# A two-layer relational graph network on one core: edge rows issued by ScalarE, a third stream written as plain blocks, and x halves ahead of the blocks

## The chip, the core and the metric

The kernel runs on one core of one Trainium2 chip. Five engines of the core matter here: TensorE (PE; its weight loads are PEld), VectorE (DVE), ScalarE (ACT), GpSimd (POOL) and SyncE (SP). Sixteen DMA engines move data between HBM and the on-chip memories for all of them. The metric is the device time of one execution in microseconds, and lower is better.

## The reference

Inputs: `x` (50000 x 128), 50000 edges with source `src`, destination `dst` (sorted), a type out of 8 and a row of attributes, and per layer eight weight matrices, a root matrix, a bias and batch-norm parameters.

```python
def _rgcn_edge_conv(h, xe, src, dst, etype, w, rt, b):
    m = jax.nn.relu(h[src] + xe)
    seg = etype * n + dst
    sums = segment_sum(m, seg, R * n)
    cnt = segment_sum(ones, seg, R * n)
    mean = sums / maximum(cnt, 1.0)[:, None]
    out = einsum('rnd,rdo->no', mean.reshape(R, n, -1), w)
    return out + h @ rt + b

h = maximum(_layernorm(x), 0.0)
for l in range(2):
    h = _rgcn_edge_conv(h, xe, src, dst, edge_type, weight[l], root[l], bias[l])
    h = _batch_norm(h, gamma[l], beta[l])
    if l == 0: h = relu(h)
return x + h
```

## The kernel before

**Tiles, groups, streams.** The edges are cut into 394 tiles of 127 edges. Group g (99 of them) takes one tile of each of four streams: tiles g, 99+g, 198+g and 297+g. For each group and layer: POOL gathers the source rows of each tile with an indirect DMA (L864, into one of 20 slots `hb` in layer 0, of 9 in layer 1); the group's edge rows are loaded into one of `XB` = 4 slots `xb` (`edge_rows`, L716, 256 KB); ScalarE normalises the rows (L1499, layer 0 only); VectorE adds both (L1211 in layer 0; L1214, L1215, L1217 in layer 1) and builds two selection matrices (`columns` L1228, `same_node` L1263); TensorE transposes and sorts by type (`turn`, L1749), multiplies by the weights (`products`, L1783) and sums by node (`node_sums`, L1819 and, for tiles of over 127 destination rows, L1824); ScalarE copies between (L1519, L1528, L1537), carries a node that goes on into the next tile (L1550), and copies the sums to one of `OB` = 3 slots `ob` (`sums_out`, L1562 and L1563).

**How the sums leave.** A tile's sums go to the accumulator `acc` in HBM in one of two ways. In general POOL writes 128 rows with an indirect DMA (`scatter`, L879). Where destinations are dense, a tile t covers at most `WROWS[t]` = 27/32 t + 16 rows in a row, and SP writes them as plain blocks (`window_rows`): up to 127 rows at L746, and what is beyond 127 at L749. `SPANS` lists the tiles for which that holds: 1 to 95 and 100 to 194, in the first two streams. A later block overwrites the rows that an earlier one of its stream wrote too far, so each block waits for its stream's block before to have landed (`wide_out`). `further(g)` lists the streams of a group whose tile has over 127 rows; for each, PE makes one more product (L1824), DVE one more 128 columns in L1263, and ScalarE copies 128 more columns (L1562). From group 33 on, the second stream's first block has 127 rows.

**The order of SP's queue.** In step n of a layer SP loads the first rows of group n-7's blocks into registers (`window_firsts`), issues the edge rows of group n, waits for `ob_ready` of group n-7 and issues its blocks, and then (layer 0) issues the load of half a chunk of `x` (`eh`, L766, 256 KB) that VectorE takes in the same group (L1185), and the store of the normalised half of five groups before (L730). The halves are spare work of layer 0: nearly every group from 21 on has one, before that every second. In layer 1 SP also loads chunks of 512 KB every fourth group. `sums_out` of group g waits until the blocks and scatters of group g-3 have landed.

**The loop of layer 0.** `columns` of group i+3 waits for TensorE's small products `place_column` of group i+1 (L1769), which follow `products` and, before it, `node_sums`; that waits for `same_node`, which VectorE makes after `columns`.

Of the kernel before, what the change touches and what calls it, by code (L numbers as in the profile page):

```python
# [6 lines left out]
P = 128  # L7
# [10 lines left out]
def wait(eng, sem, value):  # L18

    if value > 0:  # L20
        eng.wait_ge(sem, value)
# [20 lines left out]
def gnn_kernel(nc, x, src, dst, edge_attr, edge_type, weight, root, bias, gamma, beta, out):  # L42
    N, D = x.shape
# [6 lines left out]
    F = -(-N // (P * CW)) * CW  # L50
# [14 lines left out]
    T = P - 1  # L65
# [6 lines left out]
    NG = -(-NT // H)  # L72
# [4 lines left out]
    HB, XB, SM, OB = 20, 4, 2, 3  # L77
# [8 lines left out]
    MT, LAG = 3, 7  # L86
# [33 lines left out]
    def tiles(g):  # L120
        return [s * NG + g for s in range(H) if s * NG + g < NT]

    SPANS = ((1, NG - 4), (NG + 1, 2 * NG - 4))
    GROW, LEAST = 27.0 / 32.0, 15
    WIDE = [t for a, b in SPANS for t in range(a, b + 1)]
    WROWS = {t: int(GROW * t) + LEAST + 1 for t in WIDE}
    WB = WIDE[-1] // P + 1
# [11 lines left out]
    def in_window(g):  # L139

        return [t for t in tiles(g) if t in WIDE]
# [17 lines left out]
    with ctx:  # L159
# [509 lines left out]
        def xb_parts(g):  # L669

            ts = tiles(g)
            w = len(ts)
            if g == 0:
                return [(1, 113, 0, 1, 0), (113, P, 0, 1, 112), (0, P, 1, w - 1, T * ts[1] - 1)]
            if ts[-1] == NT - 1:
                return [(0, P, 0, w - 1, T * g - 1), (0, ENDW, w - 1, 1, T * (NT - 1) - 1)]
            return [(0, P, 0, w, T * g - 1)]

        def xb_count(gg):
            return 16 * sum(len(xb_parts(k % NG)) for k in range(gg % XB, gg + 1, XB))  # L680

        @block.sync
        def _(sp):

# [23 lines left out]
                sp.dma_start(near_i[1:P, 0:1], bass.AP(dst.tensor, FE - 1, [[FE, P - 1], [1, 1]])).then_inc(idx_in, 16)  # L708
                sp.dma_start(near_i[0:P - 1, 1:2], bass.AP(dst.tensor, FE, [[FE, P - 1], [1, 1]])).then_inc(idx_in, 16)

            def edge_rows(g, l):
                gg = l * NG + g
                wait(sp, t_ready, gg - XB + 1)
                for lo, hi, j, w, e in xb_parts(g):
                    far = bass.AP(edge_attr.tensor, e * D, [[D, hi - lo], [T * NG * D, w], [1, D]])
                    sp.dma_start(xb[lo:hi, gg % XB, j:j + w, :], far).then_inc(xb_in[gg % XB], 16)  # L716


            sp.wait_ge(blank, 4)
            for g in range(XB):  # L720
                edge_rows(g, 0)
            sp.wait_ge(inv_ready, 2)
            sp.dma_start(bass.AP(inv_tab.tensor, 1, [[F, P], [1, F]]), inv[:, :]).then_inc(inv_out, 16)
            sp.wait_ge(inv_out, 32)
# [6 lines left out]
                             eh_at(k).rearrange("p c d -> p (c d)")).then_inc(eh_out[k % ES], 16)  # L731

            def window_firsts(g):
                return {t: sp.value_load(first_i[0:1, t:t + 1], min_val=0, max_val=P * (F + WB * P - 1)) for t in in_window(g)}

            def window_rows(g, l, firsts):
                gg = l * NG + g
                for t in in_window(g):
                    s = t // NG
                    sp.wait_ge(ob_ready, gg + 1)  # L740
                    if gg > 0:
                        wait(sp, wide_out[s], 16 * windows(gg - 1, s))
                    if t - 1 not in WIDE:
                        sp.wait_ge(scat_out[(gg - 1) % OB], 16 * tiles_done(gg - 1, OB))
                    rows = min(WROWS[t], T)
                    sp.dma_start(acc[l][bass.ds(firsts[t], rows), :], ob[1:1 + rows, gg % OB, s, :]).then_inc(wide_out[s], 16)  # L746
                    if s in further(g):
                        k = H + further(g).index(s)
                        sp.dma_start(acc[l][bass.ds(firsts[t] + T, WROWS[t] - T), :], ob[0:WROWS[t] - T, gg % OB, k, :]).then_inc(wide_out[s], 16)  # L749

            sp.wait_ge(idx_ready, 1)
            for l in range(L):
                if l == 0:
                    sp.wait_ge(acc_zero[0], 16 * ZN)
                for n in range(NG):
                    if n >= LAG:
                        firsts = window_firsts(n - LAG)
                    if l > 0 or n >= XB:
                        edge_rows(n, l)
                    if n >= LAG:  # L760
                        window_rows(n - LAG, l, firsts)

                    k = early_half(n)
                    if l == 0 and k is not None:
                        wait(sp, eh_out[k % ES], 16 * (k // ES))
                        sp.dma_start(eh_at(k), bass.AP(x.tensor, half_rows(k) * D, [[CW * D, P], [1, H * D]])  # L766
                                     .rearrange("p (c d) -> p c d", d=D)).then_inc(eh_in[k % ES], 16)
                    k = early_half(n - 5)
                    if l == 0 and k is not None:
                        half_out(k)  # L770
                    for i, c in enumerate(HELD):
                        if l == 0 and n == min(HELD_SLOTS[i] + 8, NG - 1):
                            sp.wait_ge(tr_ps, HELD_SLOTS[i] + 2)
                            row_dma(sp, rows_at(0, c), x, c, held_in, True)

                    if l == 1 and n >= 8 and n % 4 == 0 and (n - 8) // 4 < len(OWN_FIRST):
                        i = (n - 8) // 4
                        if i == 0:
                            all_stored(sp)
                        else:  # L780
                            sp.wait_ge(ownT_ps, 2 * (i - 1))
                        table_dma(sp, own_at(i).rearrange("p (c d) -> p c d", d=D), h1_tab, OWN_FIRST[i], own_in[i % 2], True)

                for g in range(NG - LAG, NG):
                    window_rows(g, l, window_firsts(g))

                def node_rows(k):
                    c = ROWS[l][k]
                    s = place(l, c)
                    if l == 1:  # L790
                        sp.wait_ge(tr_ps, NG + NG - RING[1] + 2 * k + 2)
                    elif k >= SLOTS:
                        sp.wait_ge(hT_ps, turned_count(l, ROWS[l][k - SLOTS]))
                    table_dma(sp, rows_at(l, c), (hn_tab, h1_tab)[l], c, xc_in[s], True)

                if l == 0:
                    for g in range(NG - 5, NG):
                        if early_half(g) is not None:
                            half_out(early_half(g))
                    for s in range(ES):  # L800
                        sp.wait_ge(eh_out[s], 16 * len(range(s, NE, ES)))

                for k in range(SLOTS):
                    node_rows(k)

                sp.wait_ge(joined, 16 * (l + 1))
                for c in range(NC):
                    s = c % SLOTS
                    if c + AHEAD < NC and c + AHEAD in ROWS[l][SLOTS:] and l == 0:
                        node_rows(ROWS[l].index(c + AHEAD))  # L810
                    if l == 0:
                        wait(sp, sT_ps, c - RI + 1)
                        wait(sp, rows_out[c % RI], 16 * (c // RI))
                        table_dma(sp, acc_at(0, c), acc[0], c, ac_in[c % RI], True)
                    else:
                        if YI <= c < YLATE:
                            sp.wait_ge(sT_ps, NC + c - YI + 1)
                        elif YLATE <= c < YLATE + SLOTS:
                            sp.wait_ge(held_added, owns_done((4, 12, 14, 16)[c - YLATE]))
                        elif c >= TAIL + 6:  # L820
                            sp.wait_ge(sT_ps, NC + c - 1)
                        elif c >= YLATE + SLOTS:
                            sp.wait_ge(sT_ps, NC + c - SLOTS + 1)
                        table_dma(sp, acc_at(1, c), acc[1], c, y_in(c), True)
# [642 lines left out]
        def _(act):  # L1467
# [107 lines left out]
                a_.activation(own_at(k // 2)[:, k % 2 * W4:(k % 2 + 1) * W4], ps_side[:, :], ACT.Copy).then_inc(first_ready, 1)  # L1575

            for l in range(L):
                for i in range(-4, NG + 2):
                    if 0 <= i - 1 < NG:
                        carry(i - 1, l)  # L1580
                    if 0 <= i - 2:
                        sums_out(i - 2, l)
                    if l == 0 and i + 4 < NG:
                        root_of(i + 4)
                    if l == 1 and i >= 1 and own_half(i - 1) is not None:
                        first_turned(own_half(i - 1))
                    if l == 1 and i >= 2 and own_half(i - 2) is not None:
                        first_out(own_half(i - 2))
                    if 0 <= i < NG:
                        first_half(i, l)  # L1590
                    if 0 <= i + 2 < NG:
                        message(i + 2, 0, l)
                    if l == 0 and i + 4 < NG:
                        normalised(i + 4)
                    if 0 <= i < NG:
                        second_half(i, l)
                    if 0 <= i + 2 < NG:
                        message(i + 2, 1, l)
                    if l == 0 and i + 4 < NG:
                        half_normalised(i + 4)  # L1600
# [392 lines left out]
```

## Time and profile before

| | us |
|---|---|
| median of 3 runs | 2255.83 |
| lowest and highest | 2250.97 and 2261.55 |
| the profiled execution, its own time | 2256.96 |
| its span, first to last instruction | 2255.2 |

The profiled execution lies 1.1 us above the median. Layer 0's groups run from about 90 to 905 us, its dense part to 1113 us, layer 1's groups from 1113 to about 1985 us, the end of the network behind that. A busy share is an average over stages with different limits, so the stages are read apart: a step of the loop over groups is measured from one L1211 (or L1214) to the next. A step is about 7.6 to 8.6 us long in layer 0 and about 8.5 to 8.9 us in layer 1.

### The profile page before, as it was taken

To read this page: it belongs to the slowest core of one execution; us is meant where nothing else is said; L and a number is where in the kernel's file an instruction comes from. 1 tells how busy PE (TensorE), PEld (TensorE's weight loads), DVE (VectorE), ACT (ScalarE), POOL (GpSimd) and SP (SyncE) were. 2 spreads that over 40 slices of the span, in tenths; PEclk is the share of its full clock that TensorE was granted. 3 is DMA by queue.
4 is the path that set the end of the run, shared out by engine and by line. 5 is a ranking of instruction groups with operands and counts; after the bars stand their busy time and mean duration, and the time that the engine had idled before them with its cause. 6 is when DMAs were issued, how large, how long until landed. Compare 5 with 4: busy or idle time off the path is not lost. (4 is left out here: it accounts for less than half of the span.)

```text
span 2255.2 us, 59542 instructions
## 1 busy us (share of the span) xinstructions
PE 1840.5 (82%) x21976; PEld 1511.3 (67%) x21976; DVE 1500.4 (67%) x4496; ACT 1215.8 (54%) x2596; POOL 1332.8 (59%) x1235
## 2 busy tenths in 40 slices
PE   2379898888888888899788888888888888869866
PEld 1167676766766666799766666666667666769755
DVE  8778898787787776488865555555555555538554
ACT  0157788777777776344334444444444444434555
POOL 6747777666676665300177777777778787631000
PEclk8589999999999999899889999999999999989966
DMA  8824465454554554699734333333333334278699
GB/s 323 324 70 126 136 180 162 143 154 139 154 158 140 149 173 149 243 418 418 296 86 114 103 98 109 93 104 106 95 103 97 111 97 107 75 260 321 240 419 402
DMA packets 265827, 405.66 MB, mean 180 GB/s; under 512 B 35521, under 2 KB 177728, under 8 KB 265534
## 3 DMA queue, kind: packets, MB, share of 16 engines
q1 hardware_dynamic: 202232, 231.29, 31.1%
q0 software_dynamic: 41648, 90.52, 14.4%
q10 hardware_dynamic: 21654, 79.99, 8.8%
q8 instruction: 178, 2.92, 0.5%
q14 instruction: 115, 0.94, 0.1%
HBM read 255.41 MB, written 146.26 MB: 178 GB/s over the span
## 5 line engine op out<-in xcount | busy, mean ns | idle before, releaser
L879 POOL DMA_INDIRECT acc<-arena x408 | 471.4, 1155 | 243.8 <-PE ps_t L1749 125.5
L864 POOL DMA_INDIRECT arena<-h_rows,arena x394 | 437.6, 1111 | 300.3 <-DMA h_rows<-chunk_mem 180.6
L1819 PEld LDWEIGHTS ps_o<-arena 128*128 128x128 f32 x3152 | 401.9, 204 | 221.8 <-DVE arena L1263 203.6
L1819 PE MATMUL ps_o<-arena 128*128 128x128 f32 x3152 | 427.6, 292 | 146.4 <-DVE arena L1263 142.5
L864 POOL DMA_INDIRECT arena<-in_x_dram,arena x394 | 406.1, 1031 | 125.5 <-issue 118.9
L1749 PE MATMUL ps_t<-arena 128*128 128x256 f32 x1576 | 465.7, 420 | 10.7 <-DVE arena L1228 7.1
L1749 PEld LDWEIGHTS ps_t<-arena 128*128 128x128 f32 x1576 | 280.4, 198 | 97.8 <-issue 66.2
L1214 DVE TENSOR_TENSOR arena<-arena,bn_b 128x512 f32<-128x512 f32 (+1 forms) x99 | 68.7, 693 | 363.7 <-DMA arena<-h_rows,arena 363.5
L1228 DVE TENSOR_SCALAR arena<-arena 128x256 f32<-128x256 f32 x788 | 274.3, 410 | 41.0 <-PE ps_o L1769 34.5
L1263 DVE TENSOR_TENSOR arena<-arena 128x640 f32<-128x640 f32 (+2 forms) x396 | 286.8, 765 | 12.0 <-PE ps_y L1824 4.6
L1519 ACT ACTIVATE arena<-ps_t 128x512 f32<-128x512 f32 x396 | 234.3, 592 | 82.5 <-PE ps_t L1749 79.9
L1550 ACT ACTIVATE arena<-ps_o 1x512 f32<-1x512 f32 (+1 forms) x196 | 114.3, 583 | 279.1 <-PE ps_s L1824 119.1
L1783 PE MATMUL ps_y<-arena 128*32 128x128 f32 x6304 | 220.1, 282 | 29.8 <-ACT arena L1563 29.8
L1783 PE MATMUL ps_s<-arena 128*32 128x128 f32 x6304 | 226.3, 287 | 4.8 <-ACT arena L1563 4.8
L1783 PEld LDWEIGHTS ps_y<-arena 128*32 128x32 f32 x6304 | 165.0, 112 | 78.0 <-ACT arena L1563 44.0
L1499 ACT ACTIVATE arena<-arena,nmr,rstd 128x128 f32<-128x128 f32 x394 | 162.3, 482 | 78.8 <-DVE nmr L1200 76.8
L1783 PEld LDWEIGHTS ps_s<-arena 128*32 128x32 f32 x6304 | 169.0, 114 | 45.8 <-issue 24.5
L1563 ACT ACTIVATE arena<-ps_o 128x512 f32<-128x512 f32 (+1 forms) x198 | 114.2, 577 | 66.0 <-DMA acc<-arena 59.9
L1612 ACT ACTIVATE ht<-ps_t 128x512 f32<-128x512 f32 x98 | 53.0, 591 | 84.4 <-PE ps_t L1883 84.4
L1180 DVE BATCH_NORM_STATS2 st<-arena 128x6 f32<-128x128 f32 x394 | 86.0, 281 | 13.6 <-DMA arena<-in_x_dram,arena 10.0
L1957 PE MATMUL ps_t<-ident,arena 128*128 128x128 f32 x304 | 64.6, 377 | 33.9 <-ACT arena L1665 29.2
L1537 ACT ACTIVATE arena<-ps_s 128x512 f32<-128x512 f32 (+1 forms) x99 | 57.8, 584 | 55.2 <-PE ps_s L1783 55.2
(293 smaller groups left out, 2582.0 us busy)
## 6 DMA issues: line engine op xcount, KB each, us to landing
arena<-in_edge_attr_dram SPq DMA_DIRECT2D x190, 256.0 KB
chunk_mem<-acc SPq DMA_DIRECT2D x55, 512.0 KB, 12.5
acc<-arena ACTq DMA_DIRECT2D x28, 896.0 KB, 23.8
arena<-in_x_dram SPq DMA_DIRECT2D x45, 512.0 KB, 9.7
arena<-acc SPq DMA_DIRECT2D x43, 512.0 KB, 11.0
chunk_mem<-hn_rows SPq DMA_DIRECT2D x41, 512.0 KB, 11.7
out_dram<-arena ACTq DMA_DIRECT2D x38, 512.0 KB, 9.2
h_rows<-chunk_mem ACTq DMA_DIRECT2D x25, 512.0 KB, 7.0
```

Source lines behind the costliest of these rows:

```text
L864: pool.indirect_dma_start(out=hb[:, hb_slot(gg), t // NG, :], out_offset=None, in_=(x, h1_tab)[l], in_offset=at(src_t[:, t:t + 1])).then_i ...
L879: pool.indirect_dma_start(out=acc[l], out_offset=at(idx_t[:, t:t + 1]), in_=ob[:, gg % OB, t // NG, :], in_offset=None, **how).then_inc(co ...
L1180: own.mark(v.bn_stats(st6[:, j, :], hb[:, hb_slot(g), j, :]))
L1228: ins = v.tensor_scalar(pm[:, gg % 2, j, :], iota_f[:, :], slot_t[:, t:t + 1], inv_t[:, t:t + 1], ALU.is_equal, ALU.mult)
L1263: ins = v.tensor_tensor(sm[:, gg % SM, b, 0:w, :], iota_f[:, 0:P].unsqueeze(1).to_broadcast([P, w, P]), place_at[:, g, b, 0:w].unsqueeze(2 ...
L1499: ins = a_.activation(row, row, ACT.Relu, scale=rstd[:, g % 2, j:j + 1], bias=nmr[:, g % 2, j:j + 1])
L1519: a_.activation(mt_at(gg)[:, a:b, :].rearrange("p j c -> p (j c)"), ps_t[h][:, 0:(b - a) * RC], ACT.Relu).then_inc(m_ready, 1)
L1550: a_.activation(to, ps_sum[0:1, 0:w * D], ACT.Copy).then_inc(carried, 1)
L1563: a_.activation(ob[:, gg % OB, 0:w, :].rearrange("p w d -> p (w d)"), ps_sum[:, 0:w * D], ACT.Copy).then_inc(ob_ready, 1)
L1749: last = te.matmul(ps_t[h][:, (j - a) * RC:(j - a + 1) * RC], hb[:, hb_slot(gg), j, :], pm[:, gg % 2, j, :], start=True, stop=True)
L1783: last = te.matmul(product_bank(gg, b)[q * CAP:(q + 1) * CAP, j * D:(j + 1) * D], mt_at(gg)[:, j, r * CAP:(r + 1) * CAP], w_sb[l][:, r * D ...
L1819: last = te.matmul(ps_sum[:, c], sm[:, gg % SM, b, j, :], yb[:, gg % 2, b, j, :], start=b == 0, stop=b == NH - 1)
```

## The change

Three things are changed. First, the edge rows of all but layer 0's first four groups are issued by ScalarE into its own queue, at the start of step i for group i+5. Second, `SPANS` gets a third stretch, tiles 199 to 284: for groups 1 to 86 the third stream's tile leaves as two plain blocks (127 rows, and 56 to 128 more) instead of one indirect scatter; the products, columns and copies of `further` come with it, and the registers are loaded by one instruction for all streams. Third, in SP's step the x half and the store of a half stand ahead of the blocks.

```diff
-    SPANS = ((1, NG - 4), (NG + 1, 2 * NG - 4))
+    SPANS = ((1, NG - 4), (NG + 1, 2 * NG - 4), (2 * NG + 1, 2 * NG + 86))
...
+        def edge_rows(eng, g, l):
+            gg = l * NG + g
+            wait(eng, t_ready, gg - XB + 1)
+            for lo, hi, j, w, e in xb_parts(g):
+                far = bass.AP(edge_attr.tensor, e * D, [[D, hi - lo], [T * NG * D, w], [1, D]])
+                eng.dma_start(xb[lo:hi, gg % XB, j:j + w, :], far).then_inc(xb_in[gg % XB], 16)
...
             for g in range(XB):
-                edge_rows(g, 0)
+                edge_rows(sp, g, 0)
...
             def window_firsts(g):
-                return {t: sp.value_load(first_i[0:1, t:t + 1], min_val=0, max_val=P * (F + WB * P - 1)) for t in in_window(g)}
+                ts = in_window(g)
+                if not ts:
+                    return {}
+                _, values = nc.values_load_multi_w_load_instructions(
+                    first_i[0:1, ts[0]:ts[-1] + 1:NG], engines=(mybir.EngineType.SP,), min_val=0, max_val=P * (F + WB * P - 1))
+                return dict(zip(ts, values))
...
                     if n >= LAG:
                         firsts = window_firsts(n - LAG)
-                    if l > 0 or n >= XB:
-                        edge_rows(n, l)
-                    if n >= LAG:
-                        window_rows(n - LAG, l, firsts)
...
                     if l == 0 and k is not None:
                         half_out(k)
+                    if n >= LAG:
+                        window_rows(n - LAG, l, firsts)
...
             for l in range(L):
+                if l > 0:
+                    edge_rows(act, 0, l)
                 for i in range(-4, NG + 2):
+                    if i + 5 < NG and (l > 0 or i + 5 >= XB):
+                        edge_rows(act, i + 5, l)
                     if 0 <= i - 1 < NG:
                         carry(i - 1, l)
```

SP, one step in the middle of layer 0, before (the blocks of 67, 127 and 24 rows are those of group 61):

```order
L734 ISA x2
L734 TENSOR_LOAD arena
L734 ISA x2
L716 DMA arena<-in_edge_attr_dram 128x4x128
L746 ISA
L746 DMA acc<-arena 67x128
L746 ISA
L746 DMA acc<-arena 127x128
L749 ISA
L749 DMA acc<-arena 24x128
L766 DMA arena<-in_x_dram 128x512
L730 DMA hn_rows<-arena 128x512
```

The same step now, with the same group's blocks:

```order
L769 DMA arena<-in_x_dram 128x512
L732 DMA hn_rows<-arena 128x512
L753 ISA
L753 DMA acc<-arena 67x128
L753 ISA
L753 DMA acc<-arena 127x128
L756 ISA
L756 DMA acc<-arena 24x128
L753 ISA
L753 DMA acc<-arena 127x128
L756 ISA
L756 DMA acc<-arena 107x128
```

The edge rows (L716) are gone from SP, the x half (L766, now L769) and the store (L730, now L732) stand ahead of the blocks where they stood behind them, and the group has two blocks more, of 127 and 107 rows.

ScalarE, one step in the middle of layer 0, before:

```order
L1519 ACTIVATE arena<-ps_t 128x512
L1507 ACTIVATE arena<-arena,nmr,rstd 128x128 x4
L1550 ACTIVATE arena<-ps_o 1x512
L1562 ACTIVATE arena<-ps_s 128x128
L1563 ACTIVATE arena<-ps_o 128x512
```

And now:

```order
L1524 ACTIVATE arena<-ps_t 128x512
L1512 ACTIVATE spare<-spare,nmr,rstd 128x128 x4
L687 DMA arena<-in_edge_attr_dram 128x4x128
L1555 ACTIVATE arena<-ps_o 1x512
L1567 ACTIVATE arena<-ps_y 128x256
L1568 ACTIVATE arena<-ps_o 128x512
```

The issue of the edge rows stands between the normalised half and the carry, and the copy of further sums is twice as wide.

## Rows read from the trace of the kernel before

**Rows 1.** The page: busy us (share of the span) and instructions of each engine.

```profile
PE 1840.5 (82%) x21976; PEld 1511.3 (67%) x21976; DVE 1500.4 (67%) x4496; ACT 1215.8 (54%) x2596; POOL 1332.8 (59%) x1235
```

**Rows 2.** Stretches by stage: length, busy us (instructions) by engine, clock, DMA share, GB/s.

```profile
core 0: us, PE busy (x) PEld busy (x) DVE busy (x) ACT busy (x) POOL busy (x), PEclk, DMA share, GB/s
131.40:388.40 257.00, 226.48 (x3345) 179.12 (x3344) 212.00 (x926) 201.36 (x477) 186.14 (x181) 0.97 0.48 139
388.40:845.40 457.00, 382.95 (x5284) 310.30 (x5284) 362.27 (x1591) 345.98 (x848) 301.72 (x291) 0.95 0.53 151
1185.90:1390.00 204.10, 173.91 (x2220) 138.29 (x2212) 110.43 (x217) 94.74 (x171) 159.91 (x146) 0.94 0.37 106
1433.90:1904.00 470.10, 397.10 (x4917) 312.71 (x4920) 252.09 (x469) 209.04 (x416) 374.70 (x314) 0.95 0.37 101
```

**Rows 3.** One line in one stretch: one L1211 or L1214 a step.

```profile
L1211 DVE TENSOR_TENSOR arena<-arena x53: 678/691/766, 388.4 to 835.7; 128x512 f32<-128x512 f32 x53
L1214 DVE TENSOR_TENSOR arena<-arena,bn_b x53: 681/692/752, 1433.9 to 1904.0; 128x512 f32<-128x512 f32 x53
```

**Rows 4.** POOL's groups, 1434 to 1904 us: busy, mean ns of one, idle before and releasers.

```profile
L864 POOL DMA_INDIRECT arena<-h_rows,arena x209 | 231.6, 1108 | 63.7 <-issue 62.8 <-PE ps_t L1749 0.9
L879 POOL DMA_INDIRECT acc<-arena x105 | 144.3, 1374 | 32.0 <-issue 30.5 <-PE ps_t L1749 1.5
```

**Rows 5.** Waits, 1434 to 1904 us: engine, line, releaser, us in total, times, longest.

```profile
DVE arena L1214 <- DMA arena<-h_rows,arena: 218.0, 51, 6.8
ACT arena L1562 <- DMA acc<-arena: 56.4, 32, 3.7
```

**Rows 6.** VectorE's waits for x halves, 292 to 370 us.

```profile
DVE st L1185 <- DMA arena<-in_x_dram: 1.3, 3, 0.6
DVE st L1185 <- DMA spare<-in_x_dram: 0.4, 1, 0.4
```

**Rows 7.** The same waits, 380 to 860 us.

```profile
DVE st L1185 <- DMA spare<-in_x_dram: 30.7, 25, 2.3
DVE st L1185 <- DMA arena<-in_x_dram: 30.7, 20, 3.3
```

**Rows 8.** Timeline of a step in layer 0, PE and VectorE: start, length, count.

```profile
614.84 2.05 PE L1819 MATMUL ps_o<-arena 128*128 128x128 f32 x16 [0.59 <-DVE arena L1263]
616.73 0.61 PE L1824 MATMUL ps_s<-arena 128*128 128x128 f32 x4
617.27 1.08 PE L1783 MATMUL ps_s<-arena 128*32 128x128 f32 x32
618.28 0.35 PE L1769 MATMUL ps_o<-arena 128*128 128x2 bf16 x8
...
611.60 1.41 DVE L1228 TENSOR_SCALAR arena<-arena 128x256 f32<-128x256 f32 x4
613.24 1.55 DVE L1263 TENSOR_TENSOR arena<-arena 128x640 f32<-128x640 f32 x2
```

**Rows 9.** DMA view, 1653.5 to 1660 us, in 40 slices: GB/s; blocks of 64, 127, 21 rows.

```profile
GB/s 0 0 0 0 0 0 0 0 151 202 130 130 35 22 19 22 28 28 66 57 79 205 123 22 22 19 22 22 22 22 180 173 117 50 177 287 312 321 315 299
```

**Rows 10.** The same, 1679.9 to 1687.5 us: blocks of 67, 127 and 24 rows.

```profile
GB/s 0 0 0 0 19 102 218 30 22 24 22 22 22 22 24 19 22 24 19 19 86 137 194 170 89 132 326 396 410 388 410 321 410 140 119 183 240 269 302 404
```

**Rows 11.** SP's issues, timeline of those two places.

```profile
1653.63 1.11 SPq L746 DMA_DIRECT2D acc<-arena  x2
1654.95 0.63 SPq L749 DMA_DIRECT2D acc<-arena  x1
...
1679.92 0.73 SPq L746 DMA_DIRECT2D acc<-arena  x2
1680.85 2.30 SPq L749 DMA_DIRECT2D acc<-arena  x1
```

**Rows 12.** A stretch of the dense part of layer 0, columns as in Rows 2.

```profile
1020.00:1060.00 40.00, 39.78 (x359) 39.35 (x357) 33.86 (x84) 18.20 (x40) 0.00 (x0) 1.00 1.03 418
```

**Rows 13.** SP's own waits, 388 to 845 us.

```profile
SPq L746 <- ACT arena L1563: 126.6, 49, 6.1
```

More of the change, by code:

```diff
@@ L709, in _ @@
                 sp.dma_start(near_i[0:P - 1, 1:2], bass.AP(dst.tensor, FE, [[FE, P - 1], [1, 1]])).then_inc(idx_in, 16)
[L711 to L716, printed above, removed]
             sp.wait_ge(blank, 4)
             for g in range(XB):
-                edge_rows(g, 0)
+                edge_rows(sp, g, 0)
             sp.wait_ge(inv_ready, 2)
```

## The prediction

> **What bounds the kernel now.** The page says only that no engine is full: PE 82%, DVE 67%, POOL 59% [rows 1]. I therefore read the stretches by stage first, then who waits for whom, then the DMA view slice by slice.
>
> Layer 1, 1433.9 to 1904.0 us, is 53 steps [rows 3] of 8.87 us [rows 2]. POOL is busy 374.7 us of 470.1, and the gaps called issue before its indirect DMAs are 62.8 + 30.5 us [rows 2, 4]: 468 of 470 us. POOL is the bound there. VectorE waits 218 us for gathered rows, ScalarE 56 us for scatters that land late [rows 5].
>
> Layer 0, 388.4 to 845.4 us, is 53 steps [rows 3] of 8.62 us, POOL 302 us busy: not the bound [rows 2]. VectorE waits 61 us for x halves [rows 7], and a late half delays the loop between VectorE and PE. From 292 to 370 us, where there is a half in each group too, that wait was 1.7 us [rows 6]. What lies between is group 33: from there on one block has 127 rows.
>
> So the DMA view has to be read. With all sixteen DMA engines busy the core moves 418 GB/s [rows 12], 26 GB/s each. Behind the blocks of 64, 127 and 21 rows there is a burst of 151, 202, 130, 130 GB/s, then slices of 22, 19, 22, and later 22, 22, 19, 22, 22, 22, 22 [rows 9]. Behind 67, 127 and 24 rows nearly all slices from the ninth to the twentieth say 19 to 24: 12 slices of 0.19 us [rows 10]. A rate of 22 GB/s is one DMA engine, not sixteen. The 64-row block is spread, the 127-row one is not; and since 67 and 127 rows issued within 0.73 us [rows 11] run at 22 and not at 44, both are on the same engine. A row of 512 bytes at 22 GB/s takes 0.0235 us, so 127 rows hold that engine for 3.0 us.
>
> The Trainium skill, DMA: Bandwidth & Descriptors, section "Why a DMA increments its semaphore by 16 and not by 1", has the rule: a DMA from SP or ACT runs on the largest number up to 16 that divides its rows, on the lowest-numbered engines, and 127 rows run on one. By that rule the trace agrees.
>
> How full is that one engine now? In layer 0 the mean share is 0.53 of 8.62 us = 4.57 us a step for every engine [rows 2]; the blocks (215 rows x 0.0235 / 16 = 0.3) are in it, so 4.25 is other work. The blocks add 3.0 for the 127 rows and some 0.7 for the two others on this engine. That is 7.95 of 8.62 us: the fullest thing in layer 0, shown in no row of engine shares.
>
> **The change part by part.**
>
> 1. Third stream as blocks, groups 1 to 86, both layers. Removed: 86 scatters a layer, each 1.37 us plus a gap of 0.3 in layer 1 [rows 4]. POOL falls from 8.87 to 8.87 - 1.67 = 7.2 us a step and stops being the bound. Added: one product of further rows (PE 0.55 us: the one of now holds PE from 616.73 to 617.27 [rows 8]), 128 columns more in each L1263 (two, 0.13 each), 128 columns more in ScalarE's copy (0.13, beside other work).
>    Added on DMA: a block of 127 rows and one of 56 to 128. The first costs the one engine 3.0 us a step. The second costs it between 0 (spread like the 64 rows) and 92 x 0.0235 = 2.2 us (like the 67). I take 0.75, nearer the spread end, since only row counts without a useful divisor behave like 67. By the skill's rule the mean over these blocks is 33 rows, 0.8 us, which would give the same sum. So the blocks' load rises from 3.7 to 7.45 us, less 0.2 us for the scatter's share.
>
> 2. The one engine in layer 0, groups 34 to 86: 4.25 - 0.2 + 7.45 = 11.5 us a step. That counts time in which packets wait. By bytes instead, 151 GB/s x 8.62 us less 110 KB is 1.19 MB a step, over 16 engines at 26 GB/s 2.9 us, so 10.2 us. I take 10.9. The scatter, the blocks and `ob` allow three steps of slack and no more, since `sums_out` waits for the blocks of three groups before: this is a rate and is not hidden. 53 x (10.9 - 8.62) = **+121** (+84 to +153).
>
> 3. Layer 1, same groups: 0.37 x 8.87 = 3.3, less 0.3 and 0.2, plus 7.45 = 10.2; by bytes 101 x 8.87 less 110 KB gives 1.9 + 7.45 = 9.3. I take 9.7: 53 x (9.7 - 8.87) = **+44** (+23 to +70). POOL's gain is not seen there, since the one engine is later than POOL was.
>
> 4. Groups 1 to 33, second block 56 to 83 rows and no 127-row block of the second stream yet. On the one engine 5.05 us of blocks (1.35 for the first two streams' blocks, an estimate: they have 16 to 126 rows, under half of the 67 and 127 above, and most are spread; plus 3.7) and 2.5 to 3.4 of other work in layer 0: 8.0 a step against 257/34 = 7.56 now [rows 2]: **+13** (0 to +25). In layer 1: 5.05 + 1.9 to 2.7 = 7.0 to 7.7; PE has 173.9/24 = 7.25 + 0.55 = 7.8, and that ends last, against 8.5 now: **-17**. POOL's gain is seen here.
>
> 5. Groups 87 to 98: no new blocks, POOL less behind, halves earlier: -6 and **-4**.
>
> 6. x halves ahead of the blocks. Alone it would take away the 61 us of waits. But SP issues a half behind the blocks of the step before, into the same queue and onto the same engine; the time is then in the rate of item 2. Counted nothing more.
>
> 7. Edge rows by ScalarE: an issue of 0.4 us a step. In layer 0 it stands ahead of the carry; PE's further product ends 0.55 us later than now, which hides it. Without that cover: 99 x 0.4 = 40 us in layer 0. In layer 1 ScalarE is busy 209 of 470 us [rows 2]: nothing. SP's waits for `ob_ready`, 126.6 us over 49 steps [rows 13], would cover its two further issues, if these weren't held back as at 1680.85, where one took 2.30 us [rows 11]. The skill, same page, section "Issuing engines are not separate DMA queues", says that issuing from another engine saves issue time only. No row here shows two issuing queues at work in a step.
>
> Sum: 121 + 44 + 13 - 17 - 6 - 4 = **+151**. Against the profiled execution 2256.96 + 151 = 2408; its own distance to the median is 1.1 us, so 2407.
>
> **The rivals.**
>
> A. Faster: the one engine never fills. If the third stream's blocks go elsewhere, or the waits in "other work" vanish, the next limits hold. In layer 0 that is the loop: from L1819's start to L1769's end 3.79 us, L1228 to L1263 1.64, L1263 1.55, handovers 0.15 = 7.13 [rows 8], plus 0.55 + 0.27 = 7.95: 53 x 0.67 = -36, and -8 elsewhere. In layer 1 PE: 397.1/53 = 7.5 + 0.55 = 8.05 against 8.87: -43, and -23 from the other groups [rows 2]. Sum -110: 2147 us. For it: POOL's full stage. Against it: 67 and 127 rows at 22 GB/s.
>
> B. Slower still: ScalarE's issue is held as SP's was for 2.30 us [rows 11]. 2 us a step over both layers' 172 steps on top is beyond 2500 us. Against it: nothing shows that queues hold each other.
>
> C. Weak form: the engine's other work shrinks (x halves and stores find gaps) and the step is 9.5 us in layer 0 and 9.0 in layer 1: +47 + 7, less 17 and 10: 2284.
>
> D. The data do not fit and the other path is taken: no; the block limits are far from the destinations' density, and then the time would be several times as long.
>
> **How the numbers follow.** Forecast, 2330 to 2490 (items 2 to 4 at either end: +75 to +230): 0.68. C, 2268 to 2330: 0.10. A: 0.15. Within 0.5% (2245 to 2268), the two effects cancelling: 0.03. B: 0.04. The range 2245 to 2490 holds 0.81. Faster by over 0.5%: 0.15; within 0.5%, about what a measurement of this kernel can tell from no change: 0.03; slower: 0.82.
>
> **What would show it.** In the profile after: steps of 10 to 11.5 us in layer 0 from group 38 on, 9.3 to 10.2 in layer 1, with all compute engines less busy than now; ScalarE's L1562 waiting for `acc<-arena` for over 100 us in layer 0; long runs of slices at 19 to 24 GB/s; SP's second issue of a block at 2 us and over; POOL idle for PE's L1749 in layer 1. Groups 1 to 33 of layer 1 should be faster, at 7.8 us. If instead the steps in layer 0 are at 8 us and L1562 waits for nothing, the one engine was not the limit and rival A holds.

## The result, and the profile after

The changed kernel takes 2392.73 us (median of 4 runs, 2382.28 to 2398.97), the kernel before 2256.36. The ratio is 1.060 (95% interval 1.0553 to 1.0647): +136 us, slower. The forecast was 2407. The profiled execution took 2395.32 us, span 2393.6.

Stretches of the changed kernel (columns as in [rows 2]; a step is from one L1216 or L1219 to the next): groups 39 to 91 of layer 0, groups 10 to 38 of layer 1, and groups 39 to 91 of layer 1.

```profile
404.50:967.30 562.80, 433.17 (x5546) 359.28 (x5545) 375.53 (x1591) 353.18 (x848) 251.49 (x238) 0.91 0.45 128
1314.30:1536.50 222.20, 206.44 (x2759) 167.75 (x2758) 141.30 (x262) 116.89 (x234) 178.16 (x145) 1.00 0.43 119
1536.50:2036.70 500.20, 424.40 (x5208) 344.05 (x5207) 273.41 (x478) 215.62 (x419) 341.25 (x265) 0.94 0.36 101
```

The dense loop of layer 0 is 53 steps of 10.62 us where it was 8.62 [rows 2, 3]. POOL has a scatter less a step, and every engine is less busy than before as a share. In layer 1 the same groups take 9.44 us, with POOL busy 341 of 500 us: no longer the bound. Groups 10 to 38 of layer 1 became shorter, 222.2 us for 29 steps, 7.66 each, against 8.55 from the starts of before.

Where the 138.4 us between the two spans lie, from the starts of L1216 and L1219 against those of L1211 and L1214:

| piece | forecast | measured |
|---|---|---|
| layer 0, up to group 39 | +13 | +16.1 |
| layer 0, groups 39 to 91 | +121 | +105.8 |
| layer 0, from group 92 to layer 1's first group | -6 | +5.9 |
| layer 1, up to group 39 | -17 | -25.2 |
| layer 1, groups 39 to 91 | +44 | +20.2 |
| layer 1, from group 92 to the end | -4 | +15.5 |

Who waits in layer 0 (404.5 to 967.3 us; us in total, times, longest), against [rows 7]:

```profile
POOL arena L869 <- PE ps_t L1758: 225.0, 47, 11.6
...
DVE st L1190 <- DMA spare<-in_x_dram: 90.3, 30, 5.3
DVE st L1190 <- DMA arena<-in_x_dram: 74.8, 22, 6.8
```

VectorE waits 165 us for x halves instead of 61. POOL, relieved of a scatter, only waits longer for the loop. SP's own waits are all but gone, 2.6 us in this stretch where [rows 13] has 126.6:

```profile
SPq L732 <- ACT arena L1512: 1.8, 4, 0.7
SPq L732 <- ACT spare L1512: 0.8, 2, 0.4
```

SP's time goes into the issues of the further blocks instead: at L756 106 issues take 281 us in all, where 53 at L749 took 66. The same view of layer 1, 1536.5 to 2036.7 us, against [rows 5]:

```profile
DVE arena L1219 <- DMA arena<-h_rows,arena: 154.7, 53, 7.3
POOL arena L869 <- PE ps_t L1758: 82.0, 29, 7.1
...
ACT arena L1567 <- DMA acc<-arena: 79.3, 33, 6.5
```

One step of layer 0 in the timeline (start, length, what; waits in brackets), in order of time:

```profile
700.48 0.68 SPq L769 DMA_DIRECT2D arena<-in_x_dram  x1
...
701.90 0.98 SPq L753 DMA_DIRECT2D acc<-arena  x2
...
703.07 4.26 SPq L756 DMA_DIRECT2D acc<-arena  x1
...
706.00 0.87 DVE L1190 BATCH_NORM_STATS2 st<-arena 128x6 f32<-128x128 f32 x4 [5.51 <-DMA arena<-in_x_dram]
...
707.99 2.49 SPq L756 DMA_DIRECT2D acc<-arena  x1
...
711.80 3.78 PE L1828 MATMUL ps_o<-arena 128*128 128x128 f32 x16 [5.72 <-DVE arena L1268]
```

The half issued at 700.48 is in when VectorE starts on it at 706.00, 5.5 us later. Its semaphore (the counter that VectorE waits for) gets sixteen increments, which I read as one for each DMA engine; the trace's events have their times: fourteen from 703.15 to 703.77, the fifteenth at 704.41, the last at 705.97. So one engine is late, and VectorE starts when that one has landed. What is ahead of the half in SP's queue are the blocks of the step before. SP's issue of the further block takes 4.26 and then 2.49 us, against 0.63 and 2.30 in [rows 11]. PE waits 5.72 us behind VectorE. The DMA view, 700 to 710 us in 40 slices (GB/s):

```profile
GB/s 234 178 154 37 23 119 219 137 111 129 315 285 359 391 277 211 143 213 226 76 25 25 25 25 25 23 23 33 12 20 23 23 258 76 21 23 154 135 23 20
```

From the 21st slice on most say 20 to 25 GB/s: one DMA engine at work, as in [rows 9, 10], here for most of 5 us.

### The profile page after: what moved, and what is told of

Its sections match the earlier page's. It is cut to its first block and busy times, and to the rows that moved or that the text cites. A ratio compares the mean times of both kernels' runs of the same rounds, so it can differ in the third digit from the quotient of the medians.

```text
span 2393.6 us, 62259 instructions
## 1 busy us (share of the span) xinstructions
PE 1930.4 (81%) x22664; PEld 1610.7 (67%) x22664; DVE 1550.9 (65%) x4540; ACT 1240.6 (52%) x2662; POOL 1187.4 (50%) x1063
## 5 line engine op out<-in xcount | busy, mean ns | idle before, releaser
L869 POOL DMA_INDIRECT arena<-h_rows,arena x394 | 472.8, 1200 | 381.6 <-DMA h_rows<-chunk_mem 179.9
L1828 PE MATMUL ps_o<-arena 128*128 128x128 f32 x3152 | 441.6, 299 | 185.5 <-DVE arena L1268 183.3
L1828 PEld LDWEIGHTS ps_o<-arena 128*128 128x128 f32 x3152 | 420.0, 211 | 252.1 <-DVE arena L1268 223.0
L884 POOL DMA_INDIRECT acc<-arena x236 | 287.0, 1216 | 174.2 <-PE ps_t L1758 86.8
L1268 DVE TENSOR_TENSOR arena<-arena 128x768 f32<-128x768 f32 (+3 forms) x396 | 332.6, 881 | 13.5 <-PE ps_y L1833 4.6
L1219 DVE TENSOR_TENSOR arena<-arena,bn_b 128x512 f32<-128x512 f32 (+1 forms) x99 | 68.5, 692 | 273.5 <-DMA arena<-h_rows,arena 273.3
L1190 DVE BATCH_NORM_STATS2 st<-spare 128x6 f32<-128x128 f32 x192 | 41.8, 280 | 110.9 <-DMA spare<-in_x_dram 110.8
L1185 DVE BATCH_NORM_STATS2 st<-arena 128x6 f32<-128x128 f32 x394 | 86.0, 281 | 19.9 <-DMA arena<-in_x_dram,arena 16.1
```

The source lines that it names most:

```text
L869: pool.indirect_dma_start(out=hb[:, hb_slot(gg), t // NG, :], out_offset=None, in_=(x, h1_tab)[l], in_offset=at(src_t[:, t:t + 1])).then_i ...
L884: pool.indirect_dma_start(out=acc[l], out_offset=at(idx_t[:, t:t + 1]), in_=ob[:, gg % OB, t // NG, :], in_offset=None, **how).then_inc(co ...
L1268: ins = v.tensor_tensor(sm[:, gg % SM, b, 0:w, :], iota_f[:, 0:P].unsqueeze(1).to_broadcast([P, w, P]), place_at[:, g, b, 0:w].unsqueeze(2 ...
L1828: last = te.matmul(ps_sum[:, c], sm[:, gg % SM, b, j, :], yb[:, gg % 2, b, j, :], start=b == 0, stop=b == NH - 1)
```

## The experiments

Theory: blocks of 127 rows, and others whose row counts divide badly, run on one DMA engine, and that engine's 7.45 us of blocks a step set the pace. Rivals: the added computing, copying and issuing of the third stream lengthens the loop; or the order of the queues does it alone. Layer 0 and layer 1 below are us a step from group 39 to 92, from the starts of the same line in each profile. "Spread" stands for blocks whose row counts let them run on many DMA engines, "whole" for blocks as they were. The kernels ran on several chips; each ratio is to the kernel before on the same chip, whose median was 2251.07 to 2256.36 us, so a difference of a few us between two rows is not a finding.

| kernel | what it is | us (median) | ratio to before, 95% | layer 0 | layer 1 |
|---|---|---|---|---|---|
| before |  | 2256.36 | | 8.62 | 9.06 |
| after | all three edits | 2392.73 | 1.0553 to 1.0647 | 10.62 | 9.44 |
| e1_spread_after | after, blocks spread | 2114.51 | 0.9331 to 0.9419 | 7.94 | 7.82 |
| e2_spread_before | before, blocks spread | 2200.82 | 0.9712 to 0.9808 | 7.85 | 8.93 |
| e9_extra_127 | before, one more write of 127 rows | 2354.38 | 1.0388 to 1.0487 | 10.69 | 8.67 |
| e11_extra_122 | the same with 122 rows | 2305.08 | 1.0147 to 1.0275 | 9.61 | 8.85 |
| e10_extra_128 | the same with 128 rows | 2261.17 | 1.0010 to 1.0058 | 8.77 | 9.03 |
| e3_no_third | after without the third stretch | 2191.73 | 0.9699 to 0.9767 | 7.59 | 8.85 |
| e4_edges_only | only the edge rows moved | 2262.70 | 1.0016 to 1.0066 | 8.94 | 8.92 |
| e6_halves_only | only the x halves moved | 2194.77 | 0.9696 to 0.9779 | 7.68 | 9.06 |
| e5_third_only | only the third stretch | 2538.03 | 1.1227 to 1.1281 | 11.88 | 9.71 |
| e7_split_only | after, only the 127 rows cut | 2120.26 | 0.9373 to 0.9422 | 7.95 | 7.95 |
| e8_round_only | after, only the other blocks rounded up | 2264.78 | 1.0022 to 1.0066 | 9.60 | 8.43 |
| e12_spread_no_third | e3, blocks spread | 2188.41 | 0.9667 to 0.9726 | 7.68 | 8.95 |

**The same rows in other pieces, in the changed kernel.**

```diff
+    def blocks(t):
+        w = min(WROWS[t], T)
+        up = lambda n: -(-n // 16) * 16
+        mine = [(0, 112), (112, w - 112)] if True and w > 112 else [(0, up(w) if w <= 112 else w)]
+        return mine, [(0, up(WROWS[t] - T))] if WROWS[t] >= P else []
...
-                    rows = min(WROWS[t], T)
-                    sp.dma_start(acc[l][bass.ds(firsts[t], rows), :], ob[1:1 + rows, gg % OB, s, :]).then_inc(wide_out[s], 16)
-                    if s in further(g):
+                    mine, more = blocks(t)
+                    for lo, n in mine:
+                        sp.dma_start(acc[l][bass.ds(firsts[t] + lo, n), :], ob[1 + lo:1 + lo + n, gg % OB, s, :]).then_inc(wide_out[s], 16)
+                    for lo, n in more:
                         k = H + further(g).index(s)
-                        sp.dma_start(acc[l][bass.ds(firsts[t] + T, WROWS[t] - T), :], ob[0:WROWS[t] - T, gg % OB, k, :]).then_inc(wide_out[s], 16)
+                        sp.dma_start(acc[l][bass.ds(firsts[t] + T + lo, n), :], ob[lo:lo + n, gg % OB, k, :]).then_inc(wide_out[s], 16)
...
```

(Left out: the count of blocks that have to land, and the limit for the last tile, 16 rows higher.)

> The changed kernel with the same rows written in blocks that can be spread: a block of 127 rows goes as one of 112 and one of 15, every other block's row count is rounded up to a multiple of 16 (the rows too many are overwritten by the stream's next block, as before). PE, VectorE, ScalarE and POOL do what they do in the changed kernel; SP issues one DMA more for each block of 127 rows. Theory of the one engine: its 7.45 us of blocks a step fall to 0.6, nothing on DMA is full any more, and the steps come to the next limits that the prediction gave for rival A: about 8.0 us in layer 0 from group 39 on (10.6 in the changed kernel) and 8.05 in layer 1 (9.4): 2150 to 2200 us. Rival theory, the added work of the third stream (a product, columns, a wider copy, two more issues and ScalarE's issue of the edge rows) lengthens the loop: nothing of that is taken away and more is issued, so 2390 to 2430 us.

Measured: 2114.51 us, 278 below the changed kernel and 6.3% below the kernel before, and 35 us below the lower end of what was expected. Layer 0's step is as expected; in layer 1 it is 7.82 us for 8.05. The added work is all there. Its stretches of groups 39 to 91 (columns as in [rows 2]), and who waits in the first of them:

```profile
379.60:800.70 421.10, 386.35 (x5540) 314.65 (x5532) 385.01 (x1592) 352.89 (x851) 246.77 (x238) 1.00 0.60 172
1357.60:1772.10 414.50, 403.10 (x5259) 329.85 (x5258) 270.52 (x477) 215.77 (x424) 333.42 (x267) 1.00 0.46 126
```

```profile
PE ps_o L1836 <- DVE arena L1276: 34.8, 53, 0.7
```

No wait for an x half is left, SP waits 32.6 us for the sums again, and the loop between PE and VectorE runs at 7.94 us a step; PE is busy 403 of 414.5 us in layer 1. The rival of the added work falls: with all of it, both layers are faster than before.

**The same in the kernel before.** The edit is that of the first experiment.

> The kernel before with its blocks cut in the same way: 127 rows as 112 and 15, other counts rounded up to a multiple of 16. Theory of the one engine: in layer 0 the waits for x halves (61 us) go, and the step from group 39 on falls from 8.6 towards 7.6 to 8.0 us, -30 to -50 us; layer 1 stays at 8.9 us, since POOL is its bound: 2205 to 2230 us. Rival theory, the x halves wait for something else (the queue's order, bytes): no change or some us slower for one more issue a step, 2250 to 2275.

Measured: 2200.82 us, 50 less than the kernel before on that chip and slightly under what was expected. Layer 0 went from 8.62 to 7.85 us a step, layer 1 from 9.06 to 8.93. VectorE's waits for halves, expected to go, were halved: 32 us in 378.4 to 794.2 us. So the unspread blocks held the kernel before in layer 0, though not alone: the rest lies in the order of the queue, as the experiments on single edits below show. In layer 1 something else held it; that it was POOL is shown by the last experiment, where only the third stretch, a scatter less, brings the step down.

**One more write a step, of 127, 122 and 128 rows.**

```diff
+        extra_rows = dram("extra_rows", [2 * NG * P, D])
...
+                    if 41 <= n < 94:
+                        at = (l * NG + n) * P
+                        sp.dma_start(extra_rows[at:at + 127, :], ident[0:127, :]).then_inc(extra_out, 16)
```

> The kernel before with one more write of 127 rows of 512 bytes behind the blocks of each step from 41 to 93, in both layers, from a constant into memory that nobody reads; no engine but SP does more. Theory of the one engine: +3.0 us a step on an engine that has 7 to 8 of 8.6 us in layer 0 and 5.6 to 6.4 of 8.9 in layer 1: steps of about 10 us in layer 0 (+75) and 8.9 to 9.4 in layer 1 (+0 to +25): 2310 to 2370 us. Rival theory, 64 KB more among 1.3 MB a step and one more issue on SP: under +15, 2255 to 2270.

> The same added write with 128 rows in place of 127, so one row and 512 bytes more. Theory of the one engine: 128 rows are spread over sixteen, +0.19 us on each: under +15 us, 2255 to 2270. Rival theory: the same time as with 127 rows, whatever that is.

> The kernel before with the added write of 122 rows, between the 127 (+98 us) and the 128 rows (+5 to +10 us) already measured. If the number of engines is the largest one up to 16 that divides the rows, 122 = 2 x 61 go over two, 1.43 us on the fullest one instead of 3.0: between the two, 2270 to 2310 us. If only odd counts or counts by chance are kept together: as with 128 rows, 2255 to 2268. If every count that is no multiple of 16 is kept on one: as with 127 rows, 2345 to 2355.

Measured, all three inside the ranges of the theory: 127 rows 2354.38 us, +4.4%; 128 rows 2261.17 us, +0.3%; 122 rows 2305.08 us, +2.1%. One row more takes 93 us off. The median of before was 2251.07 for the first two and 2254.51 for the third: +103, +10 and +51 us. By the rate of [rows 10] the fullest engine gets 127 x 0.0235 = 3.0, 128 / 16 x 0.0235 = 0.19, and 61 x 0.0235 = 1.43 us a step; between 0.19 and 3.0, 1.43 is 44% of the way, and 51 is 44% of the way from 10 to 103. The Trainium skill's rule (DMA: Bandwidth & Descriptors, section "Why a DMA increments its semaphore by 16 and not by 1"), that the largest divisor up to 16 is the number of engines, fits these three counts; how many engines took part is read from rates and times here, not seen. VectorE's waits for halves with 127 rows (387.4 to 954.2 us), and then with 128 (385.6 to 850.6):

```profile
DVE st L1191 <- DMA spare<-in_x_dram: 99.1, 30, 5.0
DVE st L1191 <- DMA arena<-in_x_dram: 85.8, 23, 6.9
```

```profile
DVE st L1191 <- DMA spare<-in_x_dram: 35.7, 28, 2.7
DVE st L1191 <- DMA arena<-in_x_dram: 30.4, 19, 3.6
```

The cost is in layer 0 and shows at the halves, which stand behind the added write in SP's queue; in layer 1, where that engine had room, the step did not get longer (8.67 and 9.03 us against 9.06). So the price of 3.0 us on one engine is not fixed: it was about 2 us a step in layer 0 and nothing in layer 1.

**Without the third stretch.** The other two edits stay (and the registers are loaded by one instruction, here and in the next three kernels).

```diff
-    SPANS = ((1, NG - 4), (NG + 1, 2 * NG - 4), (2 * NG + 1, 2 * NG + 86))
+    SPANS = ((1, NG - 4), (NG + 1, 2 * NG - 4))
```

> The changed kernel without the third stretch: the first two streams' blocks as before, edge rows issued by ScalarE, x halves ahead of the blocks. Prediction's steps 6 and 7: together worth nothing to a few us, 2240 to 2256 us. If ScalarE's issues lay on the path (40 us without cover in layer 0): up to 2296. If the order of SP's queue alone made the halves late: -40 to -60, about 2200.

Measured: 2191.73 us, 2.7% faster than before: the case of the queue's order. VectorE's waits for halves in 379.4 to 781.6 us:

```profile
DVE st L1190 <- DMA arena<-in_x_dram: 0.2, 1, 0.2
```

0.2 us for halves instead of 61, with the same blocks on the same engine, whole, in steps of 7.59 us.

**Each of these two alone.** Edge rows issued by ScalarE alone (the third stretch is out in both kernels; here the blocks stand ahead of the halves again):

```diff
-                    if n >= LAG:
-                        window_rows(n - LAG, l, firsts)
...
                         firsts = window_firsts(n - LAG)
+                    if n >= LAG:
+                        window_rows(n - LAG, l, firsts)
```

> Of the three edits only the edge rows issued by ScalarE; two streams of blocks, x halves behind the blocks of their step. The two edits together gave 2192 us. Theory of the order: a half waits behind the 3.7 us of blocks that its own engine has before it in SP's queue, and that stands as it was: 2240 to 2260, and VectorE still waits some 60 us for halves between 388 and 845 us. Rival: the edge rows in front of the blocks filled SP's queue and its issues, so this edit alone gives most of it: 2190 to 2215 us.

Measured: 2262.70 us, no gain (ratio 1.004, just above the expected range), and VectorE waits 66.0 us for halves, as expected. x halves ahead alone (edge rows issued by SP again):

```diff
+                    if l > 0 or n >= XB:
+                        edge_rows(sp, n, l)
...
-                    if i + 5 < NG and (l > 0 or i + 5 >= XB):
-                        edge_rows(act, i + 5, l)
```

> Of the three edits only the x halves (and the stores of halves) ahead of the blocks; edge rows issued by SP. Theory of the order: a half now has the whole step's wait for the sums between itself and the blocks ahead, so VectorE's waits for halves go and layer 0 falls to 7.6 us a step: about 2195 us, and the edit by ScalarE is worth nothing without the third stream. Rival: no gain without the other edit, 2240 to 2256.

Measured: 2194.77 us against the 2195 expected; no wait for a half is left between 379.9 and 787.1 us. All of the gain of the two edits together comes from moving the half.

**The third stretch alone.** Edge rows by SP, halves behind the blocks.

> The third stretch alone: edge rows issued by SP and x halves behind the blocks as before. Theory of the one engine: the blocks' 7.45 us a step set the rate whoever issues what, so about the changed kernel's time, 2380 to 2410 us. If the other two edits had been a hindrance: under 2350. If they had hidden SP's issues, which wait for room in their queue: 2420 to 2480.

Measured: 2538.03 us, 145 slower than the changed kernel and above all three expectations, even the last. Layer 0 takes 11.88 us a step, 1.26 more than in the changed kernel. In layer 1 (1671.7 to 2186.4 us) VectorE waits for something new:

```profile
DVE arena L1224 <- DMA arena<-in_edge_attr_dram: 240.3, 51, 8.6
DVE arena L1221 <- DMA arena<-h_rows,arena: 10.5, 3, 4.4
```

The edge rows stand in SP's queue, between the blocks of two steps, and come late. But these 240 us are not the price: the waits for gathered rows fell from 154.7 to 10.5 us, and the step of layer 1 is only 0.27 us longer than in the changed kernel. Of the 149 us between the two spans 68 lie in layer 0 before group 39 (a step of groups 1 to 33 takes 9.52 us for 7.76), 67 in its groups 39 to 91 and 14 in those of layer 1. In layer 0 it is the halves that are late, 238 us from group 39 to 91 where it was 165. With three streams of whole blocks, what stands behind them in SP's queue pays. How the 145 us divide between the two edits was not run, nor whether the transfers are late or their issue, since SP's issues are held here as well.

**Which blocks.** Against the first experiment: only the blocks of 127 rows cut, then only the others rounded up. (The second stream's blocks of 113 to 126 rows, in groups 16 to 32, are cut in the one and stay as they are in the other.)

```diff
-        up = lambda n: -(-n // 16) * 16
+        up = lambda n: n
```

```diff
-        mine = [(0, 112), (112, w - 112)] if True and w > 112 else [(0, up(w) if w <= 112 else w)]
+        mine = [(0, 112), (112, w - 112)] if False and w > 112 else [(0, up(w) if w <= 112 else w)]
```

> The changed kernel with only the 127 rows cut to 112 and 15; the other blocks keep their row counts. Sizes that the prediction took: 3.0 us of one engine for a block of 127 rows, on average 0.75 for one of the others. What is left on the one engine is then some 1.5 us of blocks a step, so it isn't full: 2115 to 2150 us, near the kernel where all are spread (2114.5).

> The changed kernel with only the other blocks rounded up to multiples of 16; the blocks of 127 rows are left whole. Blocks on the one engine: 6.0 + 0.3 us a step from group 34 on instead of 7.45, 3.0 in groups 1 to 33. Steps shorter by about 1.1 us in layer 0 and 0.6 to 1.1 in layer 1 from group 34 on, by up to 0.5 before: 2393 - 58 - 45 - 10 = about 2280 us, 2260 to 2320.

Measured: 2120.26 and 2264.78 us, both inside their ranges. Cutting the 127 rows gives 272 of the 278 us; rounding the others gives 128 when it is done alone, and some 6 once the 127 rows are cut. The engine's load is what counts: below the next limit, taking more off it is worth nothing.

**Closing the square.** Two streams, spread, halves ahead, edge rows by ScalarE:

> The changed kernel without the third stretch and with the first two streams' blocks spread (127 rows as 112 and 15, the others rounded up to multiples of 16). It closes the square: with three streams 2393 us whole and 2114.5 spread, with two streams 2192 whole. Theory: with x halves ahead no step waited for the one engine any more, so spreading two streams' blocks gives little (at most the ScalarE waits for blocks): layer 0 at 7.5 us a step, layer 1 at 8.8, bound by POOL: 2175 to 2192 us. Then the third stretch is worth about -70 us where blocks are spread and +200 where they are whole. Rival: the one engine still held something with two streams, under 2165.

Measured: 2188.41 us, as expected. The third stretch costs 201 us where blocks are whole (2191.73 to 2392.73) and gives 74 where they are spread (2188.41 to 2114.51). The fastest kernel of all is the changed one with its blocks in pieces that spread: 2114.51 us.

## Why the prediction was right, step by step

**The mechanism held.** A 127-row block from SP occupies one DMA engine for 3.0 us; adding such a block a step made the kernel slower although the engine that had bound layer 1 was relieved. The experiments on row counts show it with nothing else changed, and the cut to 112 and 15 takes all of the loss away. The change's sign, its size and the groups in which most of it falls were forecast by steps that each have a measurement now. That the sum lies within 15 us of the time is partly luck: items 2 and 3 came out 39 us too high and item 5 31 us too low.

**Item 2, layer 0: 10.9 us a step, measured 10.62.** One of the two ends was wrong. The share of busy time gave 4.25 us of other work on the engine and 11.5 a step; the bytes gave 2.9 and 10.2. Without the third stretch the loop runs at 7.59 us with 3.7 us of blocks: 4.25 + 3.7 = 7.95 does not fit in that, 2.9 + 3.7 = 6.6 does. So packets' time in the trace must hold waiting as well, and the estimate by bytes is the one to use. With the halves ahead of the blocks, the kernels in which that engine is the fullest lie slightly above it:

| kernel, layer | blocks + bytes, us a step | measured |
|---|---|---|
| after, layer 0 | 7.45 + 2.9 = 10.35 | 10.62 |
| after, layer 1 | 7.45 + 1.9 = 9.35 | 9.44 |
| others rounded, layer 0 | 6.3 + 2.9 = 9.2 | 9.60 |
| others rounded, layer 1 | 6.3 + 1.9 = 8.2 | 8.43 |

With the halves behind the blocks layer 0 lies well above it: 11.88 for the same 10.35 in the third stretch alone, 10.69 for 6.7 + 2.9 = 9.6 with the extra 127 rows, and 8.62 for 6.6 in the kernel before. There the order of the queue costs on top of the load, which the estimate does not have.

**What bounded layer 0 before.** The prediction called that engine "the fullest thing in layer 0", at 7.95 of 8.62 us. That was an overstatement: by bytes its load was about 6.6. The halves were late since each stood behind the blocks of its own step in one queue, 3.7 us on one engine, and the edit that moves them, alone, took the waits away at the same load. Spreading the blocks alone took half of them away (32 us left), so both the load and the order made the halves late. Item 6 was right that this alone is worth the 61 us (60 measured) and that it is no gain on top of a rate; with three streams of whole blocks VectorE waits 165 us for halves that stand ahead of the blocks.

**Item 3, layer 1: +44, measured +20.** Two sizes were off. 9.7 us was a mean of 10.2 and 9.3, and the lower end, by bytes, was right again: 9.44. And the step of before is not 8.87 us: the 53 starts of [rows 3] from 1433.9 to 1904.0 bound 52 steps, 470.1 / 52 = 9.04. With 9.04 and 9.35 the item would have been +16. (Rival A's 397.1/53 has the same slip.) That POOL stops being the bound, and waits for PE instead, is as forecast: 82 us, against 0.9 [rows 4].

**Item 4, groups 1 to 33.** +16 for +13 in layer 0, -25 for -17 in layer 1, where a step was 7.66 us for 7.8 forecast. In that stretch there is one 127-row block a step, and POOL's gain is seen. The -17 was itself summed short: 33 steps from 8.5 to 7.8 us make -23.

**Item 5 had the wrong sign:** +21.4 us in the two tails where -10 was forecast. In layer 1, 2036.7 to 2110 us:

```profile
ACT arena L1567 <- DMA acc<-arena: 10.1, 3, 6.2
...
POOL acc L884 <- DMA acc<-arena: 9.3, 1, 9.3
```

The first scatter of the third stream waits for all blocks before it to land, and ScalarE for blocks of three groups before: so I read the queue as still full when the loop goes on; that was not shown by a run of its own. With spread blocks the tail's steps in layer 1 are 7.11 us instead of 9.74. For the tail of layer 0 the cause was not looked for further.

**Item 7, ScalarE's issue.** Next to nothing, as forecast, without the third stretch: +0.4%, 8 us, small but clear of noise. Moved together with the halves it costs nothing that can be seen (2191.73 against 2194.77 us). With the third stretch, the two edits that the prediction set at nothing are together worth 145 us: the sum was right since it was made by a rate and not by adding to before, but the same sum made for the third stretch alone would have come to 2407 too, where 2538 was measured. The Trainium skill (DMA: Bandwidth & Descriptors, section "Issuing engines are not separate DMA queues") says that issuing from another engine saves issue time only; here what stood behind held blocks in SP's queue was late by more than the issue's 0.38 us, though it wasn't tried with only the edge rows moved. The prediction hoped that SP's 126.6 us of waits would cover its further issues unless they were held as at 1680.85; they were held, and the waits fell to 2.6 us.

**The signs to look for.** Steps of 10 to 11.5 and 9.3 to 10.2, slices at 20 to 25 GB/s, a further block's issue at 2 us and over, POOL waiting for PE: all seen. One was wrong: ScalarE's L1567 hardly waits in layer 0 (it is not among the waits over 10 us), since the half, wanted in the same step, is late first. In layer 1, with no halves, it waits 79 us.

**Rival A** was given 2147 us, for the case that this engine never fills. That case did not come, but could be made: with blocks that spread, its 7.95 us a step in layer 0 were measured as 7.94, and its 8.05 in layer 1 as 7.82. The time was 2114.51 us, 33 less, nearly all of it in layer 1: -65 us in groups 39 to 91 where -43 was given, and -33 before them.

## What to carry to other kernels

Look at the row count of every DMA that SP issues before its bytes: 127 rows held one engine for 3.0 us and cost 93 us more than 128 rows over 106 steps, nearly all of it in layer 0's 53; cutting them to 112 and 15 turned a kernel 6% slower than its predecessor into one 6% faster. A mean over sixteen engines (a share of 0.5) says nothing on the fullest; slices at 20 to 25 GB/s do. What is wanted soon goes ahead of such a transfer in the queue: that alone gave 60 us here, at the same load. And where an edit trades a full engine for a transfer, make the sum as a rate of the resource that receives the work, by bytes or rows, not as a difference to before.

## What the runs showed of the hardware that was not expected

TensorE's granted clock falls in the steps with long waits, and makes them dearer. In layer 0 it is 0.91 in the changed kernel and 0.86 with the extra 127 rows, but 0.97 to 1.00 where no half is waited for (spread with the halves ahead, or without the third stretch). In the step shown above, after a wait of 5.72 us, sixteen matmuls took 3.78 us, against 2.05 in [rows 8]; the granted clock in that stretch was 0.50, the lower of the two levels, 1.2 instead of 2.4 GHz. From group 39 to 91 of layer 0 in the changed kernel 23 of 53 such groups of sixteen took over 2.5 us, each after a wait of 2 us or more; 9 others had such a wait before them and took 2.05. Together the 23 took 32 us longer than at the higher level. In the kernel before it was 12 groups and 16 us, in the spread kernel none. PE lies in the loop, so this may be part of why the measured step is 0.27 us above the estimate; that it is the cause was not shown.

SP's issue of a block is held when blocks that run on one engine stand ahead of it: at the further blocks' line an issue took 2.65 us in the middle (median of 106 in layer 0) in the changed kernel and 0.32 us with spread blocks.
